# A fused kernel's front reordered, with its first load split, and the residual transposed in 32x32 blocks by VectorE and moved by sixteen transfers

## What is computed

```python
Af, Bf = A_grid[None] * f[:, None], B_grid[None] * f[:, None]
gradv_Af  = _grad(Af[:, 0], 1) + _grad(Af[:, 1], 2)
gradvv_Bf = (_grad2(Bf[:, 0], 1) + _grad2(Bf[:, 1], 2)
             + _grad(_grad(Bf[:, 2], 2), 1) + _grad(_grad(Bf[:, 2], 1), 2))
x = jnp.maximum(f + (-gradv_Af + gradvv_Bf * 0.5) * dt[:, None, None], 0.0)
...
h = (x - mu) * rsqrt(var + 1e-05) * ln_g + ln_b            # over the features, per token
h_norm = (h - m_t) * rsqrt(v_t + 1e-08)                    # over the tokens, per feature
hyp = relu(subj_emb[subject_ids] @ hyp_w1 + hyp_b1) @ hyp_w2 + hyp_b2
gamma, beta = split(relu(hyp @ sty_w1 + sty_b1) @ sty_w2 + sty_b2)
h = h_norm * (softplus(gamma) + 1e-8)[:, None, :] + beta[:, None, :]
gates = top 2 of softmax(h @ router_w), normalised to sum 1
y = sum over 8 experts of gate_e * (relu(h @ exp_w1[e] + exp_b1[e]) @ exp_w2[e] + exp_b2[e])
return x + y
```

## Time and profile before

| | |
|---|---|
| median of 3 executions | 119.69 us (119.64 to 119.84) |
| span of the profiled execution, first to last instruction | 117.9 us |
| median less span | 1.8 us |
| PE busy | 111.9 us, 95% of the span |
| DVE busy | 91.8 us, 78% |
| ACT busy | 75.5 us, 64% |
| POOL busy | 8.8 us, 7% |
| transfers | 10.86 MB in 4583 packets |

### The profile page before, as it was taken

The page is one execution under the profiler, slowest core; times in us unless marked ns, Lnnn a source line. Parts: engine busy times, 40 slices in busy tenths (PEclk is TensorE's granted clock), DMA queues, the critical chain, the costliest instruction groups (busy, mean ns, idle before and its releaser), DMA issues.

```text
span 117.9 us, 1519 instructions
## 1 busy us (share of the span) xinstructions
PE 111.9 (95%) x506; PEld 85.0 (72%) x506; DVE 91.8 (78%) x198; ACT 75.5 (64%) x99; POOL 8.8 (7%) x18
## 2 busy tenths in 40 slices
PE   6999999998999999999999999999999999999960
PEld 2469894446646688888888888888888888888850
DVE  0398789748993496999959976996799589879781
ACT  0403456756361997777777777777777777777800
POOL 1437430000000000000000000000000000000040
PEclk9999999999999999999999999999999999999998
DMA  2999991000000270050400040021004000500004
GB/s 94 310 366 418 407 407 47 0 0 0 0 0 6 96 266 0 8 178 0 178 0 0 29 152 0 0 120 64 0 0 178 0 0 8 170 0 6 0 0 178
DMA packets 4583, 10.86 MB, mean 92 GB/s; under 512 B 800, under 2 KB 1888, under 8 KB 4576
## 3 DMA queue, kind: packets, MB, share of 16 engines
q1 hardware_dynamic: 3920, 9.93, 22.4%
q10 hardware_dynamic: 656, 0.84, 2.3%
HBM read 10.21 MB, written 0.56 MB: 91 GB/s over the span
## 4 chain that ended last, share of the span: by engine, by line
PE 84%; DVE 7%; DMA 4%; issue 1%; ACT 1%; SPq 0%; DVEq 0%
PE zt L625 11%; PE zt L626 11%; PE zt L627 11%; PE zt L614 6%; PE aux L653 6%; PE aux L650 6%; PE aux L649 6%; PE yt L653 5%; PE yt L650 5%; PE yt L649 5%; PE yt L619 4%; DMA gn<-in_grids_dram 4%; DVE st L824 2%; DVE h L853 1%; PE aux L574 1%; PE zt L543 1%
## 5 line engine op out<-in xcount | busy, mean ns | idle before, releaser
L498 ACT ACTIVATE hid_hi<-zt,pv 128x1024 fp32r<-128x1024 f32 x27 | 30.2, 1120 | 17.4 <-PE zt L627 17.3
L945 DVE TENSOR_TENSOR hid_lo<-hid,hid_hi 128x1024 fp32r<-128x1024 f32 x27 | 33.0, 1221 | 10.0 <-issue 5.4
L503 ACT ACTIVATE hid<-zt,pv 128x1024 f32<-128x1024 f32 x27 | 29.9, 1108 | 0.0
L625 PE MATMUL zt<-h_hi,ws 128*128 128x512 f32 x56 | 22.7, 406 | 0.0
L626 PE MATMUL zt<-h_hi,ws 128*128 128x512 f32 x56 | 21.8, 390 | 0.0
L627 PE MATMUL zt<-h_lo,ws 128*128 128x512 f32 x56 | 21.8, 389 | 0.0
L625 PEld LDWEIGHTS zt<-h_hi,ws 128*128 128x128 f32 x56 | 10.5, 188 | 3.0 <-issue 0.5
L626 PEld LDWEIGHTS zt<-h_hi,ws 128*128 128x128 f32 x56 | 10.5, 188 | 2.5 <-issue 0.5
L627 PEld LDWEIGHTS zt<-h_lo,ws 128*128 128x128 f32 x56 | 10.5, 188 | 2.2
L650 PE MATMUL aux<-hid_hi,ws 128*128 128x512 f32 (+1 forms) x32 | 12.0, 376 | 0.0
L649 PE MATMUL aux<-hid_hi,ws 128*128 128x512 f32 (+1 forms) x32 | 12.0, 376 | 0.0
(11 more groups left out here) (136 smaller groups left out, 143.0 us busy)
## 6 DMA issues: line engine op xcount, KB each, us to landing
we<-in_exp_w_dram SPq DMA_DIRECT2D x8, 512.0 KB, 9.1
gate_all<-gates_dram SPq DMA_DIRECT2D x8, 512.0 KB, 3.5
f<-in_x_dram SPq DMA_DIRECT2D x2, 256.0 KB, 4.5
ft<-in_x_exchanged_dram ACTq DMA_DIRECT2D x2, 256.0 KB, 5.3
out_dram<-acc SPq DMA_DIRECT2D x1, 256.0 KB, 2.1
out_dram<-acc SPq DMA_DIRECT2D x2, 128.0 KB, 2.0
first<-d_difference_dt_ids_dram ACTq DMA_DIRECT2D x1, 136.0 KB, 3.2
gn<-in_grids_dram SPq DMA_DIRECT2D x1, 128.0 KB, 4.4
```

The costliest lines, as they stand in the source:

```text
L498: act.activation(hid_hi[:, c, :], zt[c % 2][:], ACT.Relu, bias=bias).then_inc(hi_ready, 1)
L503: act.activation(hid[:, c, :], zt[c % 2][:], ACT.Relu, bias=bias).then_inc(hid_ready, 1)
L625: pe.matmul(zt[c % 2][:, tok], w_hi, h_hi[:, tok], start=True, stop=False)
L945: v.tensor_tensor(hid_lo[:, c, :], hid[:, c, :], hid_hi[:, c, :].bitcast(F32), ALU.subtract).then_inc(lo_ready, 1)
```

## The change

The transposition of the residual leaves TensorE and ScalarE. After the router VectorE transposes `xs` in blocks of 32 x 32 (one instruction over 128 x 1024), and SP moves the 16 blocks' rows and columns to their places in `acc` with 16 transfers; `add_up(0)` waits for all of them. The front is reordered: the first field load is split in two around the load of `gn`, the identity matrix is made by POOL and no longer loaded, POOL makes four products in another order, `rows_b` comes last and `columns_w` no longer early for the second half, the conditioning layers come elsewhere, several small VectorE chains are shortened, and the first hidden block of expert 0 is done in two parts, each as soon as half of `h` is there. The idle-time matmuls go from 9 to 7 at the start, and the 7 and 2 further on are gone. Parts of the diff (new names follow the old ones' pattern):

```diff
@@ SP
-            load(f[:, 0:BH, :], x[:, 0:BH, :], f_in[0])
+            load(f[:, 0:2, :], x[:, 0:2, :], f_in[0])
             load(gn[:], grids, gn_in)
+            load(f[:, 2:BH, :], x[:, 2:BH, :], f_second_pair_in)
             load(gt[:], gridsT, gt_in)
...
             for e in range(E):
+                if e == SLOTS:
+                    sp.wait_ge(blocks_ready, 1)
+                    for i in range(NBLK):
+                        for j in range(NBLK):
+                            to = acc[j * BLK:(j + 1) * BLK, :].rearrange("q (b i t) -> q b i t", b=B, i=NBLK)
+                            sp.dma_start(to[:, :, i, :], xs_blocks[i * BLK:(i + 1) * BLK, :, j * BLK:(j + 1) * BLK]
+                                         ).then_inc(acc_in, 16)
@@ POOL
+            step(pool.iota(col_minus_row[:], pattern=[[1, P]], base=0, channel_multiplier=-1,
+                           allow_small_or_imprecise_dtypes=True))
+            pool.tensor_scalar(ident, col_minus_row[:], 0.0, None, ALU.is_equal).then_inc(ident_ready, 1)
...
-            product(u_b0, f, gn[:, 1, :]).then_inc(b0_ready[1], 1)
...
-            product(u_a1, ft, gt[:, 1, :]).then_inc(a1_ready[1], 1)
-            product(u_b1, ft, gt[:, 0, :]).then_inc(b1_ready[1], 1)
+            product(u_a1, ft, a1_grid).then_inc(a1_ready[1], 1)
...
+            product(u_a0, f, a0_grid).then_inc(a0_ready[1], 1)
+            product(u_b1, ft, b1_grid).then_inc(b1_ready[1], 1)
+            product(u_b0, f, b0_grid).then_inc(b0_ready[1], 1)
@@ ACT
-            act.dma_start(ident, identity).then_inc(ident_in, 16)
...
-                act.activation(lv2[:, batches(n)], ve2[:, batches(n)], ACT.Ln).then_inc(lv2_ready, 1)
+                act.activation(lv2[:, batches(n)], mv2[:, batches(n), 1], ACT.Ln, bias=eps_tok[:, 0:1],
+                               scale=gsq[:, 0:1]).then_inc(lv2_ready, 1)
...
             embedded()
-            relu_step(0)
-            relu_step(2)
             hyper_first()
+            relu_step(0, 2)
+            relu_step(2, 1)
+            relu_step(3, 1)
             hyper_second()
...
             inverse_sd_tokens(0)
-            transposed_step(0)
             conditioned(0)
@@ PE
+            def layer1_0_first(n):
+
+                if n == 1:
+                    pe.wait_ge(hid0_ready, 1)
+                h_of = h[:, half(n)].rearrange("p (k u j) -> p u k j", k=2, u=2)
+                z_of = z0[0].rearrange("p (k u j) -> p u k j", k=2, u=2)
+                for u in range(2):
+                    pe.wait_ge(h_ready, 2 * n + u + 1)
+                    pe.wait_ge(h_act_ready, 2 * n + u + 1)
+                    last = pe.matmul(z_of[:, u], we[:, 0, 0, 0, :], h_of[:, u], start=True, stop=True,
+                                     skip_group_check=True)
+                last.then_inc(z0_ready, 1)
@@ DVE
             v.wait_ge(gn_in, 16)
-            product(u_a0, f, 0, gn[:, 0, :]).then_inc(a0_ready[0], 1)
...
+            v.wait_ge(p128_in, 16)
+            v.tensor_scalar(gsq[:], ln_g, ln_g, 0.25, ALU.mult, ALU.mult).then_inc(gsq_ready, 1)
+            v.tensor_scalar(minus_half_g[:], ln_g, -0.5, None, ALU.mult).then_inc(gsq_ready, 1)
             v.wait_ge(f_in[1], 16)
             product(s_b2, f, 1, b2_grid).then_inc(s_ready[1], 1)
...
-            product(u_a0, f, 1, gn[:, 0, :]).then_inc(a0_ready[1], 1)
...
             router()
+            v.wait_ge(xs_ready, B)
+            v.transpose(xs_blocks[:].rearrange("p b j -> p (b j)"),
+                        xs[:].rearrange("p b j -> p (b j)")).then_inc(blocks_ready, 1)
...
-                        v.wait_ge(acc_ready, HALVES)
+                        v.wait_ge(acc_in, 16 * NBLK * NBLK)
```

More of the change, by code:

```diff
@@ L34 @@
 SLOTS = 2
-HALF_DIFF2, IDENT = range(2)
 DIFF_AT = P
@@ L545, in step_cross, with rows_a @@
                     last.then_inc(rT_ready, 1)
-            def rows_a(n, start):
+            def rows_a(n):
                 pe.wait_ge(a0_ready[n], 1)
@@ L687, in _ @@
             step_cross(0, 1)
-            rows_a(0, start=True)
+            rows_a(0)
             pe.wait_ge(diff2_in, 16)
-            rows_b(0, 0, start=False)
-            rows_b(0, 1, start=False)
-            columns_b(0)
-            columns_w(0, 0, final=True)
-            columns_w(0, 1, final=True)
+            rows_b(0, final=False)
             pe.wait_ge(onehot_ready, 1)
@@ L697, in _ @@
             net_layer(0, pw[0:NS, EMB_AT:EMB_AT + SE], onehot[:], SE)
-            step_cross(1, 0)
+            columns_b(0, 0)
+            columns_b(0, 1)
             net_layer(1, pw[:, HW1_AT:HW1_AT + SH], se[:], SH)
-            step_cross(1, 1)
-            rows_b(1, 0, start=True)
+            columns_w(0, 0, final=True)
+            columns_w(0, 1, final=True)
             pe.wait_ge(p128_in, 16)
             net_layer(2, pv[:, HW2_AT:HW2_AT + SH], hyp1[:], SH)
-            rows_b(1, 1, start=True)
+            step_cross(1, 0)
+            step_cross(1, 1)
             net_layer(3, pv[:, SW1_AT:SW1_AT + SE], hyp2[:], SE)
-            columns_w(1, 0, final=False)
+            rows_a(1)
             pe.wait_ge(net_sb, 4)
@@ L710, in _ @@
                       stop=True).then_inc(net_ps, 1)
-            columns_w(1, 1, final=False)
-            pe.wait_ge(ident_in, 16)
+            pe.wait_ge(ident_ready, 1)
             pe.wait_ge(xp_ready, BH)
             norm_transposed(0)
-            columns_b(1)
-            step_transposed(0)
-            rows_a(1, start=False)
-            keep_warm(WARM_H[0])
-            wait_for_h(0)
+            columns_w(1, 0, final=False)
+            columns_w(1, 1, final=False)
+            columns_b(1, 0)
+            columns_b(1, 1)
+            rows_b(1, final=True)
             pe.wait_ge(net_sb, 6)
-            pe.wait_ge(acc_ready, 1)
             pe.wait_ge(w_in[0], 16)
-            for c in range(C):
+            layer1_0_first(0)
+            for c in range(1, C):
                 layer1_0(0, c)
             layer2_0(0, 0)
-            layer2_0(0, 1)
             pe.wait_ge(xp_ready, B)
             norm_transposed(1)
+            layer2_0(0, 1)
             layer2_0(0, 2)
             layer2_0(0, 3)
-            step_transposed(1)
             logits(0)
-            keep_warm(WARM_H[1])
-            wait_for_h(1)
-            for c in range(C):
-                if c == C - 1:
-                    pe.wait_ge(acc_ready, HALVES)
+            layer1_0_first(1)
+            logits(1)
+            for c in range(1, C):
                 layer1_0(1, c)
-                if c == 0:
-                    logits(1)
             pe.wait_ge(ld_ready, 1)
```

209 lines of the change are left out of this document (111 added, 98 removed).

## The result

The changed kernel takes **125.59 us** (124.53 to 126.99, 4 executions), the kernel before 119.66 (119.60 to 119.84) beside it: a ratio of 1.046 (1.040 to 1.051), 5.9 us slower by the medians where 1.7 us less was forecast. The ratio leaves out the slow, profiled execution; by it the loss is 5.5 us. The four times scatter by 2.5 us and follow the clock: the two executions with a mean granted clock of 0.956 took 126.99 and 126.18, the two at 0.982 and 0.979 took 125.00 and 124.53. The kernel before scatters by 0.2 here, and by up to 1.3 in the larger sets further on (119.00 to 120.33 over 29, two outliers in another set aside).

A forecast was written before the change was run, and what follows sets the result against it. TensorE was taken to run seven experts without a gap after the front, so the end is the front's end plus a constant. Gains of 0.57 and 1.14 make 1.71 us: 119.69 - 1.7 = 118.0 us, own range 117.2 to 118.7.

The forecast's parts named there:

- At 0.43 the last is issued at 46.65 and ... landed at 48.8: SP's 16 residual transfers: issued 0.43 us each from 40.20, in time for add_up(0) at 49.05, costing zero.
- Rival (a): Sixteen transfers late, add_up(0) holds VectorE, then TensorE; at 0.667 each 2.3 us come back, 120.3 us; 10%.
- the slack behind the sum: Behind add_up(0), VectorE's low part is done at 54.47, TensorE reads it at 55.50: 1.0 us before TensorE waits.
- u_a0 is late by 0.35 to 1.3. I take 0.7: First half's start: u_a0 waits for the second pair of f; 0.35 from the product, 0.35 from later landing.
- Rival (b): Clock rises late at the start; rows_a to columns_w cost up to twice, 119.9 us with half at low level; 9%.
- The field was forecast at 11.0: First half: neg_xp starts at 11.0 us, 1.1 after the earlier 9.91, from the later stencil and two conditioning layers.
- Together 0.7 less: First half, field to transposes: savings of 0.35, 0.1 and 0.25 us; transposes end at 16.1.
- So TensorE comes last: Ahead of expert 0: h's first pair is ready at 18.8, TensorE's work ends at 19.0; 0.57 us gained.
- The order leaves no gap here, so I cost the dropped filling at nothing: Ahead of expert 0: real work replaces the seven filling matmuls, so removing them costs zero.
- Second half, 1.14 gained: Expert 0 and second half: residual transposes (0.44) and a stretch (0.98) removed, 0.08 and 0.2 us added; no wait for h.
- The block transposition of 1.2, hidden: VectorE's residual transposition takes 1.2 us inside an idle stretch of 3.41 before the first hid_lo.
- the 1.7 us of gain: Whole kernel: 0.57 us before expert 0 plus 1.14 in the second half, 1.71 off the span.

The follow-up runs named there:

- e10: The old-front kernel e2 with each residual transfer halved, 32 transfers of 128 pieces for 16 of 256; 135.68 us (one execution).
- e9: e2 with 12 matmuls on zeros in TensorE's wait for expert 2's low part; 123.02 us, ratio 1.026 to the kernel before.
- e15: e12 with the first half's field in two loads around gn's, as in the change; 119.50 us, ratio 0.997 to the kernel before.
- e17: e12 again, measured beside e15 on the same chip; 118.75 us, ratio 0.992 to the kernel before.
- e1: The changed kernel with the residual transposed by TensorE and copied by ScalarE as before; 121.36 us, ratio 1.016 to the kernel before.
- e3: The changed kernel with block transposition in two parts in the second half's statistics and the 16 transfers issued from 25 us; 119.80 us, ratio 1.002.
- e7: e3 with the first half's field in one load and 9 matmuls on zeros at the start; 118.78 us, ratio 0.992 to the kernel before.
- e12: e7 with 3 matmuls on zeros ahead of the first half's xn transposes and 3 ahead of expert 0; 118.71 us, ratio 0.990.
- e2: The kernel before with only the residual changed: block transposition after the router, sixteen late transfers; 124.86 us, ratio 1.045.
- e5: e1 with 9 matmuls on zeros at the start in place of 7; 121.46 us (120.20 to 121.81), ratio 1.012 to the kernel before.

## Why the prediction was wrong

- **"At 0.43 the last is issued at 46.65 and ... landed at 48.8": this step failed, and it decided the result.** The sixteen issues stand 0.65 to 0.67 apart, 3.5 us more by the last, and that one landed 1.0 later than assumed. The row of 0.43 was a store from SBUF to DRAM; I took "small pieces of 128 bytes" as what makes transfers alike. e10 shows that the pieces don't matter. The upper bound of 0.667, from the same rows, was near the truth by luck: it was the longest issue of a weight load, not a row of such moves. Rival (a) gave the place, the victim and the point of decision ("from about 0.63 each") correctly, and the measured pace is over that point. It had 10%.
- **Rival (a)'s price was too small**: 2.3 us of wait were forecast, 3.3 came (the issues and the landing; the slack behind the sum, 1.0 in the forecast, was 4.5 less 3.3, so near). The clock behind the wait wasn't in it at all: about 2 by e9, 2.85 in the profiled execution. I had written the clock down as a rival of its own at the start of the kernel, and didn't ask what a wait of 3 us further on does to it.
- **"u_a0 is late by 0.35 to 1.3. I take 0.7"**: in e15, whose clock is full, the field is 0.7 later than in e17, 0.75 in the time. The term was right. In the changed kernel itself `u_a0` started at 6.76, 1.2 late, near the upper end.
- **Rival (b) had the right place and the wrong course.** It let the clock come late. In the changed kernel it was up behind the wait of 1.73 (0.71 for four matmuls at 6.90) and then fell: 0.57 of clock from 8 to 12 us. In e1's profiled execution it did come late, at about 10.5. The field was forecast at 11.0 and came at 13.36; in e3's execution at full clock it came at 11.71, at which 0.39 was a wait for `neg_half_diff`. Its chance of 9% was too small, and it varies by the execution.
- **"Together 0.7 less"** (field to the transposes' end, 5.8 before): 5.17 in the changed kernel, 5.44 in e7, so 0.6 and 0.3 less. Right in the first, half in the second.
- **"So TensorE comes last"** failed: `h` came last. From the transposes' end to expert 0 it was to take 2.9 us instead of 3.9; it took 3.47 (18.53 to 22.00). TensorE's real work was done at 21.19, 2.66 behind the transposes, and it waited 0.81 for `h`. From the first token statistics to `h` the shorter chain saved 0.22 (2.87 for 3.09), where 0.35 and 0.3 of overlap were taken.
- **"The order leaves no gap here, so I cost the dropped filling at nothing"**: the gap was there, as the line above says. The cost of the dropped filling in it was nothing in this execution: the granted clock is 1.00 from 12 to 54 us. What it costs in others isn't shown (e7 against e12).
- **Second half, 1.14 gained**: 1.28 by the profile. Right, and `h` wasn't waited for, as forecast. The block transposition of 1.2, hidden: right.

With the transfers on time (e3) the change takes 119.80, the time of the kernel before and not the forecast 118.0. So the one failed step cost 5.3 to 5.8 us, and the 1.7 us of gain failed by themselves, by the clock, the late `h` and the load. About 1.0 of them is real, and e12 and e17 have it (118.7 us): the same arithmetic and the same two ideas, with the transfers issued 16 us earlier, one first load, two more matmuls on zeros at the start, and filling in two places.

## What to carry to other kernels

Count transfers before bytes: a queue of many small moves costs its issues one after the other on the engine that issues them, so start them as soon as their data exist, or let a second idle engine issue half. Take the price of one from a transfer with the same ends, and where the trace has none, give the highest row as much weight as the nearest. A late operand can cost twice on TensorE, the wait and the half clock behind it (3.3 and about 2 us here); put a price on both. And where matmuls on zeros are removed "because real work covers them", work out when each operand is there, as the order of the instructions doesn't show the waits.

## What the runs showed of the hardware that I had not expected

- An issue of a move from SBUF to SBUF over 32 partitions takes 0.60 to 0.61 us of SP's queue with 128 or with 256 pieces of 128 bytes, 0.65 to 0.67 from start to start; the store of the gate from SBUF to DRAM over as many partitions takes 0.43. POOL takes 0.58, on its own queue and at the same time.
- Splitting 16 transfers into 32 added 10.8 us.
- Behind a wait of about 3 us TensorE worked at the low pace for 3.1 us in one execution (e2) and for 5.7 in another (the changed kernel).
- Nine executions of one kernel lay in two groups 1.2 us apart (e5: 120.2 to 120.5 and 121.4 to 121.8), with nothing changed in the code; the slower ones have the lower mean granted clock (0.983 to 0.986, against 0.992 to 0.996).
